# A decoder layer on one core: all feed-forward weights are turned at the end of cross attention, and two copies change places in the attention step

## What is computed

```python
x = x + _L0_attn_ref(_layernorm(x), W_qkv, W_z, W_b, W_a, conv_w, ...)   # gated delta rule, 16 value heads
x = x + _L0_xattn_ref(_layernorm(x), ctx, ctx, Wc, bc)                   # cross attention, 16 heads, 4 groups
x = x + _L0_ffn_ref(_layernorm(x), w_gate, w_up, w_down)                 # the weights and inputs rounded

def _L0_ffn_ref(x, w_gate, w_up, w_down):         # H = 512, I = 2048
    gate = _mx_linear(x, w_gate)
    up = _mx_linear(x, w_up)
    inter = jax.nn.silu(gate) * up
    return _mx_linear(inter, w_down)

def _mx_linear(x, w):                             # blocks of 32 share an exponent; both sides are rounded
    return jnp.einsum('bsh,oh->bso', _q_act(x), _q_w(w))
```

## Time and profile before

| | us |
|---|---|
| median of 3 runs | 2153.07 (2152.37 to 2153.5) |
| the profiled execution, as timed | 2152.93 |
| its span, first to last instruction | 2151.2 |
| cross attention, from the first step's scores to the end of the block | about 1470 to 1937 |
| feed-forward, to the end | 1937 to 2151 |

### The profile page before, as it was taken

The page is one execution under the profiler, slowest core; times in us unless marked ns, Lnnn a source line. Parts: engine busy times, 40 slices in busy tenths (PEclk is TensorE's granted clock), DMA queues, the critical chain, the costliest instruction groups (busy, mean ns, idle before and its releaser), DMA issues. The chain is left out here.

```text
span 2151.2 us, 54777 instructions
## 1 busy us (share of the span) xinstructions
PE 2012.7 (94%) x19308; PEld 1462.8 (68%) x19308; DVE 1701.6 (79%) x3949; ACT 1506.5 (70%) x4257; POOL 697.2 (32%) x602
## 2 busy tenths in 40 slices
PE   6799999999999999999999999868999999878998
PEld 3577777777777777777777777656666666544453
DVE  8777878878878877877878888745788888866997
ACT  2678788878888888887888888735666666563342
POOL 6411121121121112112111211213677777762332
PEclk9899999999999999999999999969999999998999
DMA  4000000000000000100100101133333333141111
GB/s 106 30 11 30 21 20 25 25 20 20 30 10 29 30 10 24 35 10 11 48 10 10 45 25 38 35 116 90 97 108 102 107 106 111 62 153 57 50 61 44
DMA packets 119589, 105.88 MB, mean 49 GB/s; under 512 B 12096, under 2 KB 94016, under 8 KB 119488
## 3 DMA queue, kind: packets, MB, share of 16 engines
q1 hardware_dynamic: 119488, 104.77, 15.8%
HBM read 70.66 MB, written 34.08 MB: 49 GB/s over the span
## 5 line engine op out<-in xcount | busy, mean ns | idle before, releaser
L769 PE MATMUL proj<-xn_hi,w_lo 128*128 x744 | 350.5, 471 | 0.0
L771 PE MATMUL proj<-xn_hi,w_hi 128*128 x744 | 293.8, 395 | 0.0
L770 PE MATMUL proj<-xn_lo,w_hi 128*128 x744 | 292.5, 393 | 0.0
L1175 DVE SCALAR_TENSOR_TENSOR qkv<-conv_in,taps,qkv 128x512 f32<-128x512 f32 x372 | 269.3, 744 | 0.0
L1422 POOL TENSOR_TENSOR o_scale<-o_var,neg_half 128x4 f32<-128x4 f32 x66 | 66.5, 1024 | 527.8 <-DVE o_var L1205 527.7
L1438 POOL TENSOR_TENSOR k_len<-sumsq,pos_half 128x4 f32<-128x4 f32 x31 | 45.4, 1464 | 555.8 <-DVE sumsq L1363 555.8
L1303 DVE TENSOR_TENSOR i_less_r<-bank_c,join_mask 128x256 f16<-128x256 f32 x320 | 120.6, 418 | 93.9 <-PE bank_c L832 93.2
L1085 ACT ACTIVATE inv<-bank_b 128x256 f16<-128x256 f32 x320 | 108.0, 382 | 87.2 <-PE bank_b L853 83.8
L771 PEld LDWEIGHTS proj<-xn_hi,w_hi 128*128 128x128 f32 x744 | 139.9, 188 | 32.5
L1030 ACT ACTIVATE g_mask<-mask_ge,g_cols 128x128 fp32r<-128x128 f32 x512 | 153.3, 408 | 8.4 <-DVE g_cols L1395 8.4
L1958 ACT ACTIVATE probs_t<-ps_s 128x512 f32<-128x512 f32 x128 | 69.6, 596 | 126.8 <-PE ps_s L1780 126.6
(11 more groups left out here) (328 smaller groups left out, 5778.3 us busy)
## 6 DMA issues: line engine op xcount, KB each, us to landing
out_t<-o_out SPq DMA_DIRECT2D x66, 256.0 KB, 2.0
w_hi<-out_t SPq DMA_DIRECT2D x32, 512.0 KB, 5.6
w_raw<-in_L_attn_W_qkv_dram SPq DMA_DIRECT2D x32, 256.0 KB, 2.9
wq_dram<-wq_q SPq DMA_DIRECT2D x48, 128.0 KB, 2.5
x_sb<-in_x_dram SPq DMA_DIRECT2D x16, 256.0 KB, 2.7
w_raw<-in_L_attn_W_z_dram SPq DMA_DIRECT2D x16, 256.0 KB, 2.7
w_raw<-in_L_attn_W_out_dram SPq DMA_DIRECT2D x16, 256.0 KB, 2.7
x_in<-in_x_dram SPq DMA_DIRECT2D x16, 256.0 KB, 6.1
```

Of the source, the lines that this page charges most:

```text
L769: pe.matmul(out, w_lo[:, k, cols], sh.xn_hi[:, k, tok], start=(k == 0), stop=False)
L770: pe.matmul(out, w_hi[:, k, cols], sh.xn_lo[:, k, tok], start=False, stop=False)
L771: product = pe.matmul(out, w_hi[:, k, cols], sh.xn_hi[:, k, tok], start=False, stop=(k == KT - 1))
L1175: dve.scalar_tensor_tensor(out=out, in0=conv_in[:, j, :, k:k + T], scalar=taps[:, j, k:k + 1], in1=out, op0=ALU.mult, op1=ALU.add).then_in ...
```

## The change

Four things are done.

1. In every attention step ACT copies the turned probabilities at place (0, 1) first and the keys behind them. PE has one piece of the projection less at place (0, 0), and one more at (0, 1), behind `mix`.
2. `load_rows` is cut in two: the first three 512 KB loads go out one chunk earlier.
3. The eighth piece of the weights is loaded at the end of cross attention, into the place of rows that are already turned, and its three groups are turned there: 24 groups for 21. Ten of the 24 are copied by DVE, fourteen by ACT. `turn(0)` now stands behind the last `spread` and `mix`. The store of the last chunk goes ahead of the stores of the last tokens. The first tile of rounded tokens is loaded there too, into a dead part of `gate_up_rows`.
4. `feed_forward` loses its identity copy, the wait for the first tokens' load, both late loads, the three late groups and their copies.

```diff
+        self.ident_b = ctx.enter_context(nc.sbuf_tensor("ident_b", [P, P], BF16))
+        self.first_tokens = self.gate_up_rows[:, 1, 0, :]
...
+        GROUPS_T = [(b, part) for b in range(EARLY) for part in U] + [(b, 2) for b in range(EARLY)] + [(EARLY, i) for i in range(3)]
+        BY_DVE = [t for t in range(len(GROUPS_T)) if t in (1, 3, 9) or t >= 12 and t % 5 in (0, 2, 4)]
...
+                    if not after:
+                        load_first_rows()
                     chunk(b, 3, after)
...
                 store_chunk(B - 1, CHUNKS - 2)
+                store_chunk(B - 1, CHUNKS - 1)
+                for u in U:
+                    sp.wait_ge(wq_dma[u], 16 * B * CHUNKS // 2)
+                sp.wait_ge(turned_ps, 4)
+                sp.dma_start(carried.gate_up_rows[:, 0, :, :], wq_steps_dram[:, EARLY, 0:4, :]).then_inc(late_in, 16)
+                sp.dma_start(down_rows[:, EARLY, :, :], wq_steps_dram[:, EARLY, 4:6, :]).then_inc(late_in, 16)
+                sp.wait_ge(xq_dma[0], 16)
+                sp.dma_start(carried.first_tokens, xq_dram[0]).then_inc(tokens_in, 16)
...
-                            for piece in range(done, done + (2, 1, 1, 3, 2, 3, 2, 2)[2 * c + u]):
+                            done = pieces((1, 1, 1, 3, 2, 3, 2, 2)[2 * c + u])
...
                             if before or c + u:
                                 mix(*last_tile(b, c, u))
+                            if (c, u) == (0, 1):
+                                done = pieces(1)
...
                         pe.wait_ge(pt1_done[t - 1], GROUPS * B)
                     else:
-                        pe.wait_ge(turned_done, t - 2)
+                        pe.wait_ge(*turned_by(t - 3))
+                    b, part = GROUPS_T[t]
+                    if b == EARLY:
+                        pe.wait_ge(late_in, 32)
...
                 turn_probs(B - 1, GROUPS - 1, 1)
-                turn(0)
                 spread(B - 1, 1)
                 mix(B - 1, GROUPS - 1, 1)
-                for t in (1, 2):
+                for t in (0, 1):
                     turn(t)
                 combine(B - 1, 0)
-                for t in (3, 4):
+                for t in (2, 3):
                     turn(t)
...
+                            if before or c + u:
+                                turned(*last_tile(b, c, u))
                             if before and (c, u) == (0, 1):
                                 keys(b, 1)
-                            if before or c + u:
-                                turned(*last_tile(b, c, u))
...
-                load_tokens(0, 0)
-                sp.dma_start(wq_gu[:, :, :], wq_steps[:, LATE, 0:4, :]).then_inc(wgu_in, 16)
-                sp.dma_start(wq_down[:, :, :], wq_steps[:, LATE, 4:6, :]).then_inc(wd_in, 16)
+                sp.sem_inc(xq_in[0], 16)
```

More of the change, by code:

```diff
@@ L1645, in load_rows @@
                         sp.wait_ge(wq_dma[u], 16 * EARLY * CHUNKS // 2)
-                    for b in range(EARLY - 1):
+                    for b in range(3):
+                        sp.dma_start(carried.gate_up_rows[:, b, :, :], wq_steps_dram[:, b, 0:4, :]).then_inc(rows_in, 16)
+                def load_rows():
+                    for b in range(3, EARLY - 1):
                         sp.dma_start(carried.gate_up_rows[:, b, :, :], wq_steps_dram[:, b, 0:4, :]).then_inc(rows_in, 16)
@@ L1833, in step, with pieces @@
                                 turn_probs(*last_tile(b, c, u))
-                            for piece in range(done, done + (2, 1, 1, 3, 2, 3, 2, 2)[2 * c + u]):
[L1835 to L1839, removed]
+                            def pieces(count):
+                                for piece in range(done, done + count):
+                                    if piece < PIECES and after:
+                                        project(b + 1, piece, piece + 1)
+                                    elif piece >= PIECES and further:
+                                        project(b + 2, piece - PIECES, piece - PIECES + 1)
+                                return done + count
+                            done = pieces((1, 1, 1, 3, 2, 3, 2, 2)[2 * c + u])
                             if before and (c, u) == (0, 0):
@@ L2030, in weights_turned @@
                     act.wait_ge(turned_ps, t + 1)
[L2031 to L2038 removed]
+                    place, bank = turned_places(t)
+                    act.activation(place, bank, ACT.Copy).then_inc(turned_act, 1)
                 turned(B - 1, GROUPS - 1, 1)
@@ L2042, in _ @@
                 act.wait_ge(y_ps[1], B)
-                mixed(B - 1, 0)
-                weights_turned(0)
-                mixed(B - 1, 1)
-                for t in range(1, 3 * EARLY):
-                    weights_turned(t)
+                for u in U:
+                    mixed(B - 1, u)
+                for t in range(len(GROUPS_T)):
+                    if t not in BY_DVE:
+                        weights_turned(t)
             @block.vector
@@ L2255, in _, with weights_turned @@
                 reciprocals(B - 1, 1)
+                def weights_turned(t):
+                    dve.wait_ge(turned_ps, t + 1)
+                    place, bank = turned_places(t)
+                    dve.tensor_copy(place, bank).then_inc(turned_dve, 1)
                 for u in U:
@@ L2259, in _ @@
                 chunk(None, 0)
-                for u in U:
-                    finish(B - 1, u)
-                    token_variance(B - 1, u)
+                dve.wait_ge(y_ps[1], B)
+                weights_turned(1)
+                finish(B - 1, 0)
+                token_variance(B - 1, 0)
+                weights_turned(3)
+                finish(B - 1, 1)
+                token_variance(B - 1, 1)
                 token_norms(B - 1)
                 token_scales(B - 1)
+                weights_turned(9)
                 token_rounds(B - 1)
+                for t in BY_DVE[3:]:
+                    weights_turned(t)
             @block.gpsimd
@@ L2500, in turn_tokens @@
                     pe.wait_ge(xqt_done, 2 * m + u)
+                    tokens = carried.first_tokens if isinstance(m, int) and m + u == 0 else x_q[u][:, :]
                     for k in range(KT):
-                        last = pe.transpose(ps_x[:, k, :], x_q[u][:, P * k:P * k + P], ident[:, :])
+                        last = pe.transpose(ps_x[:, k, :], tokens[:, P * k:P * k + P], ident[:, :])
                     last.then_inc(xq_ps, 1)
@@ L2539, in slot @@
                         if this:
-                            if isinstance(m, int) and 2 * m + u == 0 and c == CH - 1:
-                                for part in range(2):
-                                    turn_weights(part)
-                                for part in range(2):
-                                    pe.wait_ge(wt_done[part], 1)
                             gate_up(m, u, c)
```

89 lines of the change are left out of this document (24 added, 65 removed).

## The result

| | us |
|---|---|
| changed kernel, median of 4 runs | 2132.72 (2131.97 to 2133.91) |
| kernel before, beside it, 4 runs | 2152.72 (2151.55 to 2153.5) |
| ratio, with its 95% interval | 0.9912 (0.9899 to 0.9924) |
| the changed kernel once more, 5 runs | 2134.73 (2133.07 to 2139.32) |
| its profiled execution and span | 2132.07 and 2130.4 |

20.0 us are saved, against 16.6 forecast. To see where, both traces are cut at five places which every version of the kernel has: the scores of step 1; the last turned probabilities (the last `turn_probs`); the first transposes of the feed-forward layer; the third column of slot 1; and the eight transposes of rounded inner values in front of PE's last long wait.

What follows compares the result with a forecast made beforehand. PE was taken to bound the attention steps, DVE close behind; elsewhere the bound changes between engines. 2152.93 - 2.9 - 5.0 - 2.1 - 8.6 + 2.0 = 2136.3, with 0.14 added 2136.5 us; range 2130.5 to 2143.

Steps and rivals of the forecast that it cites:

- Steps: Attention steps: combine starts 0.55 us earlier in six steps, the last step loses 0.4 us; 2.9 us saved.
- End of cross attention: End of cross attention: earlier row loads and copies shared by DVE and ACT save 5.0 us, with 24 groups for 21.
- Between the blocks: Before the feed-forward layer: first tokens already in place, so PE's start behind ACT's end shrinks from 2.42 to 0.3; 2.1 saved.
- Slot 0: Feed-forward slot 0: first transposes to DVE's fifth product take 15.2 us instead of 23.8 at full clock; 8.6 us saved.
- The clock: PE's clock falling at its start, in slot 0 or at the last spread; 2.0 us charged.
- (a): Steps and clock: DVE is not late, steps give 6.8 us, clock stays up; 2130.6 us, chance 0.18.
- (b): Steps give nothing, the 0.4 us loss stays, the clock falls at two or three places for 4 us; 2141.8, chance 0.25.
- (c): End of cross attention: late rows become the bound, block ends 10 us later than forecast; 2146.5 us, chance 0.04.
- (d): Steps: the clock falls in each of six for 6.8 us at half clock, costing 20.4 us; 2156.9 us, chance 0.03.
- The rule on the shared port: Steps: DVE and GpSimd lock a shared port pair; one collision more or fewer per step means 6.5 us either way.

Runs made afterwards that it cites:

- rows_undone: Changed kernel, but all row loads go out at the old place and the first group is turned ahead of the last spread, as before; 2138.38 us.
- act_copies_all: Changed kernel, but ACT copies all 24 groups at the end of cross attention and DVE none; 2140.54 us.
- tokens_in_ff: Changed kernel, but the first tile of tokens is loaded at the start of the feed-forward layer, as before; 2139.0 us.
- busy_all: Changed kernel plus products nobody reads in PE's long waits: the last slot, late attention steps and slot 1 of the feed-forward layer; 2133.68 us.
- rebalanced: Changed kernel with groups 2 and 4 turned earlier, eight DVE copies instead of ten, group 0 copied between mix_hi copies, last step's keys first; 2137.18 us.
- after_again: The changed kernel run once more, word for word; 2134.73 us.
- late_in_ff: Changed kernel, but the eighth piece of the weights is loaded, turned and copied in slot 0 of the feed-forward layer, as before; 2139.05 us.
- busy_ends: Changed kernel with products nobody reads in PE's long waits, including behind the last turned group and the feed-forward layer's first transposes; 2131.75 us.
- steps_only: Kernel before with both step edits only: ACT copies probabilities ahead of keys, and one projection piece stands behind mix; 2147.58 us.
- act_order_only: Kernel before with only ACT's order in the steps changed, turned probabilities ahead of the keys; 2153.07 us.
- piece_only: Kernel before with only one piece of the projection moved behind mix, ACT's order unchanged; 2151.79 us.
- busy_tail: Changed kernel plus 18 products nobody reads in the last slot, where PE waits for POOL; 2131.87 us.

## Why the prediction was right, and where it was off

The time fell in the range, 3.8 us below the forecast (2.6 below by the median of all nine runs of the changed kernel, 2133.91). Of these 3.8 us 2.0 are the charge for the clock. Most of the rest is luck, since the start and the end alone differ by 2.2 us in the two traces. Term by term:

- **Steps, 2.9 forecast, 3.7 measured.** The mechanism is as told: `mix` waits for `mix_lo` (0.50 us for 0.65), `combine` 0.53 us earlier for 0.55, the period 55.01 instead of 55.63, the last step's loss 0.42 for 0.4. The term was mis-sized since the first of the six steps gained 0.96 and the others 0.62, and the 0.55 looked at `combine` alone. What the prediction never asked is what each of the two edits does without the other; the two runs show that it would have been wrong about both.
- **End of cross attention, 5.0 forecast, 4.6 measured.** Moved by the 5.06 us, the spread is at 1907.48 (1907.35 forecast), the first combine at 1910.48 (1910.3), DVE's second residual at 1918.06 (1917.95), the rounding at 1924.42 (1924.35), DVE's last seven copies from 1925.86 (1925.85), the end at 1932.46 (1932.0). Only the last twelve groups took longer, since ACT stood idle for 1.66 us while PE waited for DVE's copy behind the rounding. rows_undone confirms the part of the row loads together with the first group's place, and act_copies_all that of the second engine.
- **Between the blocks, 2.1 forecast, 2.0 measured** (0.46 us behind ACT's end for 0.3). tokens_in_ff shows that it is worth more than its own wait: 3.4 and 2.7.
- **Slot 0, 8.6 forecast, 8.4 measured.** From the first transposes to DVE's fifth product 15.4 us for 15.2, PE's wait 2.53 for 2.7.
- **The clock, +2.0 forecast, 0 and 0.8 measured.** This is the step that failed: "I charge 2.0". None of the three places it named had a fall in the changed kernel. The sum without the charge, 16.6 + 2.0 = 18.6 us, is what the pair of traces gives for A to C (3.71 + 6.52 + 8.40 = 18.63); the other 2.2 us of their difference are the start and the end. The size was not foolish for a single fall: one of 3.4 us at the layer's start costs 1.7 (C 17.79 in busy_all), one of 6.8 costs 2.35 (C 18.46). But the charge took the waits of 1.5 and 2.7 us as likely to have one, on the strength of the single 2.46 us of the earlier trace rows. Over all runs the first had a fall in three of seven traces and the second in two of seven (last section). At 1.7 us for the first, and some 0.2 to 0.4 for the second (C 17.95 in rebalanced against 17.79 in busy_all, 18.84 in tokens_in_ff against 18.46 in act_copies_all), an estimate from these rows is 0.8 us, to which a fall in the steps like that of after_again may come. So the charge was too large, and that the changed kernel's first trace had none of them is luck.
- **The rivals.** (a), 2130.6, had the clock right and DVE wrong; DVE is late. (b) is out, the steps gave 3.7. (c) is out: the late rows were issued at 1914.20 and no group waited for them. (d) is out: the only low stretches in its steps are two of 3.4 us (1852.2 to 1855.6 and 1865.9 to 1869.3), in its last two, where the kernel before had them too. Its price was also too high. It took 6.8 us of low clock for each fall, and the one behind the 2.46 us of the earlier trace rows is 3.4 us long (1870.9 to 1874.3).
- **The rule on the shared port.** The long ones among the 48 operations of the earlier trace rows are 22 after and 21 before, so no collision more in each step, and the 6.5 us either way, which the prediction had worked out for one collision by the rule of the Trainium skill (SBUF — State Buffer, "Who interferes with whom"), did not come. Whether it is this lock that makes them long, no run here shows.

## What to carry to other kernels

An edit that moves a copy ahead of another moves the wait to whoever needs the second one; it pays only with work that lies in front of that reader, so try the halves of such a change apart before trusting the sum. Cut a span at fixed places of the program and compare the pieces: where the clock falls at the same places they repeat to 0.1 us, while the whole time wanders by several. Do not add up what the parts cost when they are undone one by one: late_in_ff, tokens_in_ff, act_copies_all and rows_undone lose 5.5, 6.1, 6.3 and 3.7 us in B and C, 21.7 in all, where all of it together gained 14.9, in part because each of them brings a clock fall of its own. And price a wait of PE at its length and, where it is long, at the slower products behind it as well; a few products that nobody reads in such a wait can take that second part away.

## What was not expected of the hardware

The wait in front of the feed-forward layer's first transposes, and the low stretch of PE's clock that began within 3 us of them. In all kernels but busy_ends PE waits again behind these transposes, for 0.7 to 1.1 us, so the first wait is not alone.

| kernels | wait, us | low stretch, us |
|---|---|---|
| before, steps_only, act_order_only, piece_only, tokens_in_ff | 4.4 to 4.95 | 6.8, in all five |
| act_copies_all | 2.53 | 6.8 |
| after, after_again, rows_undone, busy_tail | 1.52 | none |
| busy_all | 1.52 | 3.4 |
| late_in_ff, rebalanced | 1.38, 1.20 | 3.4 |
| busy_ends | 0.45 | none |

Above 2.5 us the clock fell here each time (six traces, only one of them near 2.5), and it began to fall while PE was still in that wait. Between 1.2 and 1.5 us it fell in three of seven traces, 0.9 to 1.9 us behind the start of the transposes. There the wait alone does not decide, and a forecast can give a chance, not a value. The 2.5 us ahead of slot 1 had a fall in tokens_in_ff and in rebalanced, and none in five other traces.
